# Preparation of a latent-attention layer: six small loads asked behind the compressing weights, and result remainders computed ahead of the splitting of values

## Chip, cores and metric

The kernel runs on 1 core of one Trainium2 chip. The metric is the device time of one execution in microseconds; a kernel's time is the median of its runs.

## What is computed

One layer on 2048 tokens of 512 features in fp32: latent attention with 16 heads, then a linear layer, each followed by a sum with its input and a layer normalisation. Cut to what matters:

```python
cq = rms_norm(x @ w_qa.T, q_a_ln_w)                 # 384 compressed query features
q  = (cq @ w_qb.T), 16 heads of 128 + 64; the 64 are rotated by cos, sin
ckv = x @ w_kva.T                                   # 128 + 64 features
k_pe = rotate(ckv[..., 128:])                       # one rotated key of 64 for all heads
ckv_l = rms_norm(ckv[..., :128], kv_a_ln_w)
kv = ckv_l @ w_kvb.T                                # per head 128 of key, 128 of value
attn = softmax(mask(q @ k.T * scale)); y = (attn @ v) @ w_o.T
x = layernorm(x + y)
x = layernorm(x + (x @ (weight * scale_weight[:, None]).T + bias))
```

The kernel never forms `kv`: it folds `w_kvb` into the query weights and into the output weights, so keys are `ckv_l` (`key_c`) with the rotated `key_pe`, and values are `ckv_l` without its weight (`val`). Each fp32 operand is kept as two parts, the rounded value (hi) and its remainder (lo), and products are made of the parts.

## The kernel before

`build` runs `prepare_phase`, then `attention_phase`. The preparation walks over four chunks `c` of 512 tokens; a chunk has four tiles `t` of 128 tokens, and the folding of one of four groups of heads goes on beside the tiles. On every engine the order is written out by hand; engines meet through counting semaphores.

**Before the chunks.** SyncE (SP) asks for the identity, the compressing weights `wa_rows` (`w_qa`, then 128 rows of `w_kva`, lines 260 and 261, semaphore `wa_loaded`), the tail of `w_kva` (262), chunk 0's angles `cos` and `sin` (`load_angles`, 255), the two norm weights `q_w` and `kv_w` (264, 266), the mask (268) and the FFN's scale (269). GpSimd (POOL) asks for the first tile of tokens, waits for `wa_loaded`, then asks for the second tile, `w_kvb`, `w_qb` (285, 287), two tiles and the output weights. TensorE (PE) waits for `ident` and `wa_loaded` and turns the compressing weights (354, 358); ScalarE (ACT) and VectorE (DVE) copy them out. DVE then casts the mask (584), scales the norm weights (588, 590) and waits for the angles (592); ACT waits for four such steps, `consts_made`, before its first squares (535).

**A tile on each engine.** PE: `project` (392), `turn_x` of the next tile (370), then a few `fill`s of the weight folding (436, 442, 447, 452, 459), between them `project_key` (402), and `turn_results` of the tile before (410, 412, 417); three more fills (`at_end`, 459) and `turn_results(3)` end a chunk. ACT: squares (535, 537), copy of the tokens, `split` hi parts (506, 517, 519), `cq_n` (544), then `hi(t-1)`, the rounding of the turned results into `cq`, `key_c` and `key_pe` (528, 530, 528), and its stores to DRAM (550, 553, 561, 565). DVE: `safe` (621), rotation of the key (631 to 637), remainders of the folded weights (`split`, 601, 603), `c_n` (644), the splitting of the values (`v_hi` 650, `v_lo` 652), and for `t > 0` `lo(t-1)`, the three remainders of the results (611, 613, 611). POOL: the powers (309), the FFN scaling (321) and the loads of the next chunk.

**What waits for `lo`.** The three operations of `lo` count `tok_lo`. PE's `project_key(t)` waits for `3 * (t - 1)` of the chunk, since it overwrites the bank from which `lo` reads; so `project_key(2)` waits for `lo(0)`, which DVE computes in tile 1. `turn_results(3)` waits for `lo(2)`, computed in DVE's tile 3. The store of `cq` (565) waits for `lo(3)`; ACT's `hi(0)` of the next chunk waits for that store's landing (`cq_free`), since it writes into the same `cq`. Nobody in the preparation reads `val`; the attention does.

```python
for t in range(4):
    ...                                   # rotation, split(n) for the tile's fills
    dve.wait_ge(cqn_done, c * 4 + t + 1)
    ...                                   # c_n, then v_hi and v_lo
    if t:
        lo(t - 1)
for n in at_end:
    split(n)
lo(3)
```

Of the kernel before, what the change touches and what calls it, by code (L numbers as in the profile page):

```python
# [39 lines left out]
def chunk(c):  # L40

    return c


def stored(view):

    return view.bitcast(F32)
# [67 lines left out]
def prepare_phase(nc, m, block, x, w_qa, w_kva, w_qb, w_kvb, w_o, q_ln, kv_ln, w_ffn, scale_w, ident_in, mask_in, cos_in, sin_in):  # L115
# [6 lines left out]
    with ExitStack() as ctx:  # L122
        def sem(name):
            return ctx.enter_context(nc.semaphore(name))
# [45 lines left out]
        wa_loaded = sem("wa_loaded")  # L170
# [80 lines left out]
        @block.sync  # L251
        def _(sp):
            def load_angles(c):
                for table, source in ((cos, cos_in), (sin, sin_in)):
                    sp.dma_start(table[:, 4 * chunk(c):4 * chunk(c) + 4, :],
                                 source.rearrange("(t p) d -> p t d", p=P)[:, 4 * chunk(c):4 * chunk(c) + 4, :]
                                 ).then_inc(angles_loaded[c > 0], 16)

            sp.dma_start(m.ident[:, :], ident_in).then_inc(ident_loaded, 16)
            sp.dma_start(wa_rows[:, 0:3, :], w_qa.rearrange("(o p) i -> p o i", p=P)).then_inc(wa_loaded, 16)  # L260
            sp.dma_start(wa_rows[:, 3, :], w_kva[0:C]).then_inc(wa_loaded, 16)
            sp.dma_start(wa_tail[0:DR], w_kva[C:C + DR]).then_inc(tail_loaded, 16)
            load_angles(0)
            sp.dma_start(q_w, q_ln.rearrange("(k p) -> p k", p=P),
                         allow_slow_non_contiguous=True).then_inc(wo_free, 16)
            sp.dma_start(kv_w, kv_ln.rearrange("(k p) -> p k", p=P),
                         allow_slow_non_contiguous=True).then_inc(cq_free, 16)
            sp.dma_start(mask, mask_in).then_inc(wq_free, 16)
            sp.dma_start(ffn_scale, scale_w.rearrange("(o p) -> p o", p=P), allow_slow_non_contiguous=True
                         ).then_inc(m.ffn_free, 16)  # L270
            sp.wait_ge(x_loaded[3], 16)
            for c in range(1, NCH):
                load_angles(c)


            sp.wait_ge(cq_free, 16 * 2)
            load_tokens(sp, m, 1)
# [294 lines left out]
        @block.vector  # L572
        def _(dve):
            nc.vector.memset(minus_half, -0.5).then_inc(consts_made, 1)
            for k in range(1, KH, 2):
                dve.wait_ge(wa_turned, k + 1)
                nc.vector.tensor_copy(wa_t[:, k, 0:QLR + C], m.bank[4 + k]).then_inc(wa_copied, 1)
            dve.wait_ge(wa_turned, KH + 1)
            nc.vector.tensor_copy(wa_t[:, :, QLR + C:WA], TR[:, 0:KH * DR].rearrange("p (k n) -> p k n", k=KH)
                                  ).then_inc(wa_copied, 1)  # L580
            dve.wait_ge(ident_loaded, 16)
            nc.vector.tensor_copy(m.ident16[:, :], m.ident[:, :]).then_inc(consts_made, 1)
            dve.wait_ge(wq_free, 16)
            nc.vector.tensor_copy(m.mask16[:, :], mask).then_inc(consts_made, 1)

            dve.wait_ge(wo_free, 16)
            dve.wait_ge(cq_free, 16)
            nc.vector.tensor_scalar(q_w, q_w, SCALE, None, ALU.mult).then_inc(consts_made, 1)
            dve.wait_ge(m.ffn_free, 16)
            nc.vector.tensor_scalar(ffn_scale, ffn_scale, -1.0, None, ALU.mult).then_inc(ffn_negated, 1)  # L590
            dve.wait_ge(consts_made, 4)
            dve.wait_ge(angles_loaded[0], 32)
            nc.vector.memset(m.small[:, 60:61], 0.0).then_inc(tok_lo, TOK)
            nc.vector.memset(m.small[:, 61:62], 0.0).then_inc(split_lo, SPLITS)
            with dve.Fori(0, NCH) as c:
                def split(n):
                    if fills[n][0] != "turn":
                        src, dst, scale = split_places(n)
                        dve.wait_ge(split_hi, c * SPLITS + split_of[n] + 1)
                        if scale is None:  # L600
                            nc.vector.tensor_tensor(dst(1), src, stored(dst(0)), ALU.subtract).then_inc(split_lo, 1)
                            return
                        nc.vector.scalar_tensor_tensor(out=dst(1), in0=src, scalar=scale, in1=stored(dst(0)),
                                                       op0=ALU.mult, op1=ALU.subtract).then_inc(split_lo, 1)

                def lo(t):

                    for n, (src, dst, scale) in enumerate(token_places(c, t)):
                        dve.wait_ge(tok_hi, c * 12 + 3 * t + max(n, 1) + 1)
                        if scale is None:  # L610
                            nc.vector.tensor_tensor(dst(1), src, stored(dst(0)), ALU.subtract).then_inc(tok_lo, 1)  # L611
                        else:
                            nc.vector.scalar_tensor_tensor(out=dst(1), in0=src, scalar=scale, in1=stored(dst(0)),
                                                           op0=ALU.mult, op1=ALU.subtract).then_inc(tok_lo, 1)

                for t in range(4):
                    b = t % 2
                    tile = chunk(c) * 4 + t

                    dve.wait_ge(squared, c * 8 + 2 * t + 2)  # L620
                    nc.vector.tensor_scalar(safe[:, 2 * b:2 * b + 2], means[:, 2 * b:2 * b + 2], RMS_EPS, None,
                                            ALU.add).then_inc(eps_added, 1)
                    dve.wait_ge(key_ready, c * 4 + t + 1)
                    if t == 3:
                        dve.wait_ge(angles_loaded[1], 32 * (NCH - 1))
                    kp = KP.rearrange("p (a d) -> p a d", a=2)
                    cos_t = cos[:, bass.ds(tile, 1), :].broadcast_to([P, 2, HALF])
                    sin_t = sin[:, bass.ds(tile, 1), :]
                    tc = t_cos.rearrange("p (a d) -> p a d", a=2)
                    ts = t_sin.rearrange("p (a d) -> p a d", a=2)  # L630
                    nc.vector.tensor_tensor(tc, kp, cos_t, ALU.mult).then_inc(rope_parts, 1)
                    nc.vector.tensor_tensor(ts[:, 0:1], kp[:, 1:2], sin_t, ALU.mult).then_inc(rope_parts, 1)
                    nc.vector.tensor_tensor(ts[:, 1:2], kp[:, 0:1], sin_t, ALU.mult).then_inc(rope_parts, 1)
                    dve.wait_ge(rope_parts, c * 12 + 3 * t + 3)
                    kr = k_rot[b].rearrange("p (r a d) -> p r a d", r=2, a=2)
                    for a, op in ((0, ALU.subtract), (1, ALU.add)):
                        nc.vector.tensor_tensor(
                            kr[:, :, a, :], tc[:, a:a + 1, :].broadcast_to([P, 2, HALF]),
                            ts[:, a:a + 1, :].broadcast_to([P, 2, HALF]), op).then_inc(krot_done, 1)
                    for n in beside[t]:  # L640
                        split(n)

                    dve.wait_ge(cqn_done, c * 4 + t + 1)
                    nc.vector.tensor_scalar(c_n[b], PROJ[b][:, QLR:QLR + C], rstd[:, 2 * b + 1:2 * b + 2],
                                            None, ALU.mult).then_inc(cn_done, 1)
                    dve.wait_ge(cn_done, c * 4 + t + 1)
                    v_hi = m.val[:, 0, bass.ds(tile, 1), :]
                    v_lo = m.val[:, 1, bass.ds(tile, 1), :]
                    cn3 = c_n[b].rearrange("p (a d) -> p a d", a=1)
                    nc.vector.tensor_copy(v_hi, cn3).then_inc(val_hi, 1)  # L650
                    dve.wait_ge(val_hi, c * 4 + t + 1)
                    nc.vector.tensor_tensor(v_lo, cn3, stored(v_hi), ALU.subtract)
                    if t:
                        lo(t - 1)
                for n in at_end:
                    split(n)
                lo(3)
# [1374 lines left out]
```

## Time and profile before

| | |
|---|---|
| median of 3 runs | 1716.27 us (1714.79 to 1720.11) |
| the profiled execution's own time | 1716.44 us |
| its span | 1714.7 us |
| TensorE matmul busy in the span | 1679.9 us, 98% |
| DVE, ACT, POOL busy | 1380.5, 1120.8, 979.7 us |
| mean granted TensorE clock | 0.999 |

The profile is of one execution on the one core. The span runs from its first to its last instruction; the execution's own time has 1.74 us more around it. Busy time of PE includes the overlap of pipelined matmuls, so whether PE waits is read from the starts of its groups. The preparation reaches to about 143 us of the span, the attention takes the rest.

### The profile page before, as it was taken

How to read it: one execution, taken by the hardware profiler on the slowest of the kernel's cores; microseconds unless marked ns; L12 is line 12 of the kernel's file. 1: busy time of each engine (PE TensorE's matmuls, PEld its weight loads, DVE VectorE, ACT ScalarE, POOL GpSimd, SP SyncE). 2: the span in 40 equal slices, each digit the busy share in tenths (PEclk: the TensorE clock that was granted, in tenths of full speed). 3: DMA queues.
4: the chain of work that ended last, by engine and by line, in shares of the span. 5: the costliest groups of instructions: out<-in, count | busy, mean ns of one | idle time of the engine just before them, and what ended most of it. 6: DMA issues, size and time to landing. Idle time of an engine off the chain costs nothing.

```text
span 1714.7 us, 28541 instructions
## 1 busy us (share of the span) xinstructions
PE 1679.9 (98%) x8789; PEld 1395.8 (81%) x8789; DVE 1380.5 (81%) x2493; ACT 1120.8 (65%) x2128; POOL 979.7 (57%) x937
## 2 busy tenths in 40 slices
PE   7999999999999999999999999999999999999997
PEld 5567888888888888888888888888888888888775
DVE  3665788888888887878788888888888888888984
ACT  3564676666666676666677666766667777676774
POOL 4333465565555555655566555555556665556785
PEclk9999999999999999999999999999999999999999
DMA  7984322212321412223211413123123111111422
GB/s 204 367 330 136 105 68 62 87 56 88 110 80 37 144 36 81 69 80 117 81 62 44 142 50 92 51 80 114 62 66 105 56 57 62 50 44 44 136 92 80
DMA packets 112175, 164.03 MB, mean 96 GB/s; under 512 B 13600, under 2 KB 83488, under 8 KB 109984
## 3 DMA queue, kind: packets, MB, share of 16 engines
q1 hardware_dynamic: 105296, 125.86, 22.9%
q0 software_dynamic: 4864, 16.26, 3.0%
q10 hardware_dynamic: 1872, 20.19, 2.9%
q8 instruction: 68, 1.11, 0.3%
q14 instruction: 75, 0.61, 0.1%
HBM read 101.19 MB, written 61.08 MB: 95 GB/s over the span
## 4 chain that ended last, share of the span: by engine, by line
PE 89%; POOL 3%; DVE 3%; issue 2%; DMA 1%; ACT 1%; DVEq 0%; SPq 0%; ACTq 0%; POOLq 0%
PE rows L1464 35%; PE bank L1494 7%; PE bank L1497 7%; PE bank L1495 7%; PE rows L1527 7%; PE rows L1427 5%; PE bank L1527 3%; PE rows L392 2%; PE rows L1440 2%; PE bank L1427 2%; PE bank L1484 2%; PE bank L1440 1%; POOL split_p L1730 1%; PE rows L1473 1%; PE rows L1505 1%
## 5 line engine op out<-in xcount | busy, mean ns | idle before, releaser
L1730 POOL TENSOR_TENSOR split_p<-pool,split_p 128x512 fp32r<-128x512 f32 x544 | 703.3, 1294 | 503.2 <-ACT split_p L1618 503.1
L1464 PE MATMUL rows<-q_c,key_c 128*128 128x512 f32 x1632 | 477.0, 400 | 1.4 <-DVE top L1858 1.4
L1606 ACT COPY pool<-rows 128x512 f32<-128x512 f32 x480 | 281.8, 587 | 227.3 <-PE rows L1464 226.6
L1858 DVE TENSOR_TENSOR top<-rows,top 128x512 f32<-128x512 f32 x420 | 288.6, 687 | 124.5 <-ACT pool L1606 121.0
L1873 DVE TENSOR_TENSOR pool<-bank,pool 128x512 f32<-128x512 f32 x544 | 369.7, 680 | 19.8 <-PE bank L1484 19.8
L1611 ACT ACTIVATE pool<-pool 128x512 f32<-128x512 f32 x544 | 345.9, 636 | 18.1 <-DVE pool L1873 17.1
L1618 ACT CAST split_p<-pool 128x512 fp32r<-128x512 f32 x544 | 333.2, 612 | 16.7 <-PE bank L1497 16.7
L1464 PE MATMUL rows<-q_pe,key_pe 128*128 128x512 f32 x1088 | 337.1, 391 | 0.4 <-DMA q_pe<-pe_dram 0.4
L1885 DVE TENSOR_TENSOR bank<-bank,pool 128x512 f32<-128x512 f32 x480 | 330.9, 689 | 0.0
L1464 PEld LDWEIGHTS rows<-q_c,key_c 128*128 128x128 f32 x1632 | 288.0, 189 | 50.0 <-DVE top L1858 5.0
L1464 PEld LDWEIGHTS rows<-q_pe,key_pe 128*128 128x128 f32 x1088 | 204.2, 188 | 46.2 <-DMA q_pe<-pe_dram 0.9
L1497 PE MATMUL bank<-split_p,val 128*128 128x512 f32 x544 | 213.7, 393 | 2.9 <-POOL split_p L1730 2.7
L1494 PE MATMUL bank<-split_p,val 128*128 128x512 f32 x544 | 214.0, 393 | 1.5 <-ACT o_sum L1624 1.0
L1495 PE MATMUL bank<-split_p,val 128*128 128x512 f32 x544 | 212.3, 390 | 0.0
L1527 PE MATMUL rows<-wo,o_t 128*128 128x512 f32 x528 | 127.3, 390 | 0.4 <-ACT o_t L1636 0.4
L1497 PEld LDWEIGHTS bank<-split_p,val 128*128 128x128 f32 x544 | 102.1, 188 | 29.0 <-POOL split_p L1730 7.4
L1494 PEld LDWEIGHTS bank<-split_p,val 128*128 128x128 f32 x544 | 102.1, 188 | 25.9 <-ACT o_sum L1624 3.4
L1735 POOL TENSOR_TENSOR o_t<-o_sum,o_t 128x512 fp32r<-128x512 f32 x64 | 83.0, 1296 | 69.8 <-ACT o_t L1636 69.8
L1495 PEld LDWEIGHTS bank<-split_p,val 128*128 128x128 f32 x544 | 102.2, 188 | 21.2
L1527 PEld LDWEIGHTS rows<-wo,o_t 128*128 128x128 f32 x528 | 98.9, 188 | 21.7 <-issue 1.2
L1636 ACT CAST o_t<-o_sum 128x512 fp32r<-128x512 f32 x64 | 39.7, 621 | 111.4 <-DVE o_sum L1897 97.2
L1427 PE MATMUL rows<-cq,wq 128*128 128x256 f32 x612 | 80.1, 285 | 0.3 <-DVE key_pe L611 0.3
(193 smaller groups left out, 2101.9 us busy)
## 6 DMA issues: line engine op xcount, KB each, us to landing
q_pe<-pe_dram SPq DMA_DIRECT2D x128, 128.0 KB, 2.6
y_dram<-y SPq DMA_DIRECT2D x62, 256.0 KB, 2.1
cq<-cq_dram SPq DMA_DIRECT2D x19, 768.0 KB, 4.9
y<-y_dram SPq DMA_DIRECT2D x48, 256.0 KB, 3.0
pe_dram<-by_sin SPq DMA_DIRECT2D x32, 256.0 KB, 2.1
pe_dram<-by_cos SPq DMA_DIRECT2D x32, 256.0 KB, 2.2
cq_more<-cq_dram SPq DMA_DIRECT2D x10, 768.0 KB, 4.9
table<-table_dram SPq DMA_DIRECT2D x56, 128.0 KB, 2.7
```

The lines of the kernel that those rows point to most:

```text
L1464: mm = pe.matmul(by_head(out), k, q, start=(z == 0), stop=(z == 4))
L1494: pe.matmul(OUT, m.val[:, 0, j, :], split_p[:, n % 2, 0, :], start=(t == 0), stop=False)
L1495: pe.matmul(OUT, m.val[:, 1, j, :], split_p[:, n % 2, 0, :], start=False, stop=False)
L1497: pe.matmul(OUT, m.val[:, 0, j, :], split_p[:, n % 2, 1, :], start=False, stop=(t == keys(it) - 1)).then_inc(values_done, 1)
L1527: mm = pe.matmul(aux(u), o_t[:, a, h * P:h * P + P], m.wo[:, b, h, :], start=(n == 0), stop=(n == 3 * HG - 1))
L1606: nc.scalar.copy(slot(n), SCORES[n % N_SCORES]).then_inc(scores_copied, 1)
L1611: nc.scalar.activation(slot(n), slot(n), ACT.Exp).then_inc(exp_done, 1)
L1618: nc.scalar.copy(split_p[:, n % 2, 0, :], slot(n)).then_inc(p_hi, 1)
L1730: nc.gpsimd.tensor_tensor(split_p[:, n % 2, 1, :], slot(n), stored(split_p[:, n % 2, 0, :]), ALU.subtract).then_inc(p_lo, 1)
L1858: nc.vector.tensor_tensor(out, SCORES[n % N_SCORES], slot(number(it, 0)) if t == 1 else out, ALU.max).then_inc(scores_maxed, 1)
L1873: nc.vector.tensor_tensor(slot(n), MAXES, slot(n), ALU.add).then_inc(shifted, 1)
L1885: nc.vector.tensor_tensor(TOTAL, TOTAL, slot(n), ALU.add).then_inc(summed, 1)
```

## The change

Two edits, both inside `prepare_phase`. SP gets one wait, for both transfers of `wa_loaded`, ahead of `load_angles(0)`; the loads behind it on SP, `q_w`, `kv_w`, mask and FFN scale, stand behind the wait too. On DVE, `lo(t - 1)` moves from behind `v_lo` to between the wait for `cn_done` and `v_hi`. No operation is added or left out.

```diff
--- before.py
+++ after.py
@@ -260,6 +260,7 @@
             sp.dma_start(wa_rows[:, 0:3, :], w_qa.rearrange("(o p) i -> p o i", p=P)).then_inc(wa_loaded, 16)
             sp.dma_start(wa_rows[:, 3, :], w_kva[0:C]).then_inc(wa_loaded, 16)
             sp.dma_start(wa_tail[0:DR], w_kva[C:C + DR]).then_inc(tail_loaded, 16)
+            sp.wait_ge(wa_loaded, 32)
             load_angles(0)
             sp.dma_start(q_w, q_ln.rearrange("(k p) -> p k", p=P),
                          allow_slow_non_contiguous=True).then_inc(wo_free, 16)
@@ -644,14 +645,14 @@
                     nc.vector.tensor_scalar(c_n[b], PROJ[b][:, QLR:QLR + C], rstd[:, 2 * b + 1:2 * b + 2],
                                             None, ALU.mult).then_inc(cn_done, 1)
                     dve.wait_ge(cn_done, c * 4 + t + 1)
+                    if t:
+                        lo(t - 1)
                     v_hi = m.val[:, 0, bass.ds(tile, 1), :]
                     v_lo = m.val[:, 1, bass.ds(tile, 1), :]
                     cn3 = c_n[b].rearrange("p (a d) -> p a d", a=1)
                     nc.vector.tensor_copy(v_hi, cn3).then_inc(val_hi, 1)
                     dve.wait_ge(val_hi, c * 4 + t + 1)
                     nc.vector.tensor_tensor(v_lo, cn3, stored(v_hi), ALU.subtract)
-                    if t:
-                        lo(t - 1)
                 for n in at_end:
                     split(n)
                 lo(3)
```

SP at its start, before and then with the change (lines move by one; `small` holds `q_w`, `kv_w` and the FFN scale, `pool` the mask):

```order
L261 DMA wa_rows<-in_L_attn_w_kva 128x512
L262 DMA wa_tail<-in_L_attn_w_kva 64x512
L255 DMA cos<-const_cos 128x4x32
L255 DMA sin<-const_sin 128x4x32
L264 DMA small<-in_L_attn_q_a_ln_w 128x3x1
L266 DMA small<-in_L_attn_kv_a_ln_w 128x1
L268 DMA pool<-const_mask 128x128
```

```order
L261 DMA wa_rows<-in_L_attn_w_kva 128x512
L262 DMA wa_tail<-in_L_attn_w_kva 64x512
L255 DMA cos<-const_cos 128x4x32 [waits wa_loaded]
L255 DMA sin<-const_sin 128x4x32
L265 DMA small<-in_L_attn_q_a_ln_w 128x3x1
L267 DMA small<-in_L_attn_kv_a_ln_w 128x1
L269 DMA pool<-const_mask 128x128
```

The first load of angles now carries the wait, and the five behind it follow it in the old order.

DVE in a chunk's tile 1, from `c_n` on, before and then with the change:

```order
L644 TENSOR_SCALAR c_n<-rows,small 128x128 [waits cqn_done]
L650 ISA [waits cn_done]
L650 COPY val<-c_n 128x128
L652 ISA [waits val_hi]
L652 TENSOR_TENSOR val<-c_n,val 128x128
L609 REGISTER_ALU
L611 TENSOR_TENSOR cq<-rows,cq 128x3x128 [waits tok_hi]
L613 ISA [waits tok_hi]
L613 SCALAR_TENSOR_TENSOR key_c<-rows,small,key_c 128x128
L611 ISA [waits tok_hi]
L611 TENSOR_TENSOR key_pe<-bank,key_pe 128x128
```

```order
L645 TENSOR_SCALAR c_n<-rows,small 128x128 [waits cqn_done]
L610 REGISTER_ALU [waits cn_done]
L612 TENSOR_TENSOR cq<-rows,cq 128x3x128 [waits tok_hi]
L614 ISA [waits tok_hi]
L614 SCALAR_TENSOR_TENSOR key_c<-rows,small,key_c 128x128
L612 ISA [waits tok_hi]
L612 TENSOR_TENSOR key_pe<-bank,key_pe 128x128
L653 ISA
L653 COPY val<-c_n 128x128
L655 ISA [waits val_hi]
L655 TENSOR_TENSOR val<-c_n,val 128x128
```

The three operations of `lo` now stand in front of both operations on `val`; the two waits of `val` stay, that for `cn_done` now ahead of `lo`. Tiles 2 and 3 read the same, tile 0 has no `lo` and is as it was.

## Rows read from the trace of the kernel before

**Rows 1.** A stretch: us, busy PE, PEld, DVE, ACT, POOL, clock, DMA share, GB/s.
```profile
150.00:1600.00 1450.00, 1447.20 (x7612) 1227.76 (x7611) 1215.62 (x2049) 970.35 (x1799) 841.89 (x697) 1.00 0.25 80
```

**Rows 2.** Waits of PE from 20 to 146 us: us in total, times, longest.
```profile
PE bank L402 <- DVE key_pe L611: 2.0, 3, 1.4
...
PE rows L410 <- DVE key_pe L611: 1.5, 3, 0.6
```

**Rows 3.** DMA from 0 to 6.7 us: packets; an issue, KB, us to landing.
```profile
DMA packets 759, 1.38 MB, mean 206 GB/s; under 512 B 52, under 2 KB 180, under 8 KB 759
...
wa_rows<-in_L_attn_w_kva SPq DMA_DIRECT2D x1, 256.0 KB, 6.1
```

**Rows 4.** DMA from 6.7 to 9 us: packets.
```profile
DMA packets 2361, 0.33 MB, mean 142 GB/s; under 512 B 2172, under 2 KB 2300, under 8 KB 2361
```

**Rows 5.** DMA issue at 9.51 us: KB, us to landing.
```profile
pool<-in_L_attn_w_qb POOLq DMA_DIRECT2D x1, 768.0 KB, 7.9
```

**Rows 6.** Timeline to 20 us: start, us, engine, line, operation, idle before and releaser.
```profile
1.79 0.48 SPq L261 DMA_DIRECT2D wa_rows<-in_L_attn_w_kva  x1
...
5.67 0.49 SPq L269 DMA_DIRECT2D small<-in_L_ffn_scale_weight  x1
...
8.04 3.65 PE L354 MATMUL bank<-ident,wa_rows 128*128 128x128 f32 x16 [8.04 <-DMA wa_rows<-in_L_attn_w_kva]
...
19.26 0.49 ACT L535 ACTIVATE squares<-rows 128x384 f32<-128x384 f32 x1 [5.29 <-PE rows L392]
...
19.50 1.06 PE L436 MATMUL bank<-pool 128*128 128x128 f32 x8
```

**Rows 7.** Timeline, chunk 0, tiles 1 to 3.
```profile
28.77 1.85 DVE L637 TENSOR_TENSOR k_rot<-t_cos,t_sin 128x64 f32<-128x64 f32 x2
...
29.34 1.05 POOL L321 TENSOR_TENSOR ffn_rows<-ffn_rows,small 128x512 f32<-128x512 f32 x1
...
32.19 0.23 DVE L650 CAST val<-c_n 128x128 f32 x1
...
32.77 0.55 DVE L611 TENSOR_TENSOR cq<-rows,cq 128x384 fp32r<-128x384 f32 x1
...
32.93 0.60 PE L452 MATMUL bank<-ident,pool 128*128 128x128 f32 x4
...
33.83 1.10 PE L402 MATMUL bank<-pool,x_t 128*128 128x64 f32 x8 [0.31 <-DVE key_pe L611]
...
43.96 2.80 PE L459 MATMUL bank<-pool 128*128 128x512 f32 x6
...
47.24 2.06 DVE L603 SCALAR_TENSOR_TENSOR wo<-bank,small,wo 128x512 fp32r<-128x512 f32 x3
...
47.38 0.55 PE L410 MATMUL rows<-ident,cq_n 128*128 128x128 f32 x3 [0.61 <-DVE key_pe L611]
...
47.41 0.75 POOL L291 DMA_DIRECT2D pool<-in_L_attn_w_kvb  x1 [1.94 <-PE bank L459]
```

**Rows 8.** The chain that ended last: the store of chunk 0's `cq`.
```profile
51.78 13.73 DMA cq_dram<-cq
```

**Rows 9.** Timeline, chunk 2, then chunk 3.
```profile
96.94 0.37 ACT L530 ACTIVATE key_c<-rows,small 128x128 f32 x1
...
97.80 0.55 DVE L611 TENSOR_TENSOR cq<-rows,cq 128x384 fp32r<-128x384 f32 x1
...
129.07 0.28 DVE L611 TENSOR_TENSOR key_pe<-bank,key_pe 128x128 f32 x1
...
129.37 0.60 PE L452 MATMUL bank<-ident,pool 128*128 128x128 f32 x4
...
129.80 1.00 PE L402 MATMUL bank<-pool,x_t 128*128 128x64 f32 x8
...
139.55 2.74 PE L459 MATMUL bank<-pool 128*128 128x512 f32 x6
...
142.13 0.49 PE L410 MATMUL rows<-ident,cq_n 128*128 128x128 f32 x3
```

## The prediction

> **What bounds the kernel now.** I read, in this order, the stretches, PE's waits in the preparation, the timeline there, and the DMA traffic of the first microseconds. From 150 to 1600 us PE is busy for 1447.2 of 1450 us [rows 1]: that part keeps its length, and what the preparation gains or loses is handed to the end whole. In the preparation PE stands still at its start, until the compressing weights are in [rows 6], and then almost only at two waits, three times each, always for the last operation of `lo` (611) [rows 2]. The edits aim at just these two.
>
> **Part 1, the wait on SP.** `w_kva` is asked at 1.79 us and lands 6.1 us later, at 7.9; PE starts at 8.04, and POOL's next loads hang on the same landing [rows 3, 6]. Up to 6.7 us the DMA engines moved 1.38 MB [rows 3], which is the sum of identity, `w_qa`, 128 rows of `w_kva` and the first tile of tokens (64 + 768 + 256 + 256 KB). So going by bytes the weights could be in at 6.7; they land 1.2 us later. In between lie the six small loads: of 2361 packets from 6.7 to 9 us, 2172 are under 512 B [rows 4]. With the change these packets come after the landing. Bounds: 0 if the last engine's share of `w_kva` simply ended late, 1.2 if the small packets alone hold it back. The few packets of under 512 B before 6.7 (52 of 759 [rows 3]) say that some engines ran ahead and others were still at the large rows, so part of the 1.2 is unevenness that stays. I take **0.5**, a little under the middle. A shift of PE's start moves everything behind it, as POOL's loads start with it.
>
> That nothing of the 1.2 us is due to the small loads is the first rival; no row separates the two. The Trainium skill (DMA: Bandwidth & Descriptors, "Queues, rings and completion order") has a rule that speaks for that rival and against my term: on each DMA engine the descriptors of one issuer are consumed in ring order, so that small loads asked later on the same queue cannot stand in front of `w_kva`, and the sum below would be 1715.1.
>
> What the wait costs: six requests that ended at 6.16 us [rows 6] now start at about 7.9 - 0.5 = 7.4 and, at their old pace of 0.56 us each (seven from 2.27 to 6.16), end at about 10.7. Behind them on SP stand only angles of the later chunks, which wait for a token tile anyway. ACT needs `q_w` and mask before its squares at 19.26 [rows 6]. With a landing of up to 6.1 us [rows 3] after the request the constants are there by about 17, over 1.5 us early after the 0.5 shift: cost 0. The small packets now share the engines with POOL's loads. The one needed first is `w_qb`, asked at 9.51 and landed 7.9 us later, at 17.4 [rows 5]; PE wants it at 19.50 [rows 6]: cover of 2.1 us. Nearly all of the small packets moved within 2.3 us [rows 4], when little else was left, so the delay is at most about that, less what falls in gaps of the POOL loads: cost 0, with its excess in rival 4.
>
> **Part 2, `lo` ahead of `val`.** `v_hi` starts at 32.19 and `lo` at 32.77 [rows 7]: `lo` can start 0.58 us earlier if ACT's hi parts are there. The moved pair ends as late as `lo` ended before, so DVE's next work keeps its start. What each wait costs I take from starts. `project_key(2)` comes 0.90 us behind the four transposes in front of it (32.93 to 33.83 [rows 7]), and 0.43 where nothing is missing (129.37 to 129.80 [rows 9]): 0.47 lost. `turn_results(3)` comes 3.42 us behind three fills (43.96 to 47.38 [rows 7]), 2.58 in chunk 3 (139.55 to 142.13 [rows 9]): 0.84 lost, of which the trace counts 0.61 as idle. Rows 2 leave some 0.9 idle for chunks 1 and 2 together, 0.45 each, by starts about 0.6. Now along the chunks:
> - Chunk 0, key: all of **0.47** goes; 0.58 covers it, and PE itself is late next.
> - Chunk 0, results: 0.58 of the 0.84 goes. But this is given back. The store of `cq` is released by `lo(3)`, behind DVE's three splits from 47.24 [rows 7], which the swap doesn't move. It takes 13.73 us [rows 8], and ACT's `hi(0)` of chunk 1 waits for it, then `lo(0)`, then PE: that key wait is the longest of rows 2 (1.4) and has 0.58 more to wait. Net 0.
> - Chunk 1, key: bound by that store, no gain. DVE now computes `val` behind `lo`, which makes `safe` and POOL's power some 0.7 us late; ACT has three copies to make first, so this is hidden; without that cover it would cost the 0.7.
> - Chunk 1, results: 0.58 gained. Chunk 2, key: the next store lets ACT end `key_c` at 97.31 (96.94 + 0.37), and `lo` began at 97.80 [rows 9]. So `lo` gains only 0.49, some 0.44 with the semaphore's delay. Chunk 1's 0.58 and this wait's 0.47 together yield **0.44**.
> - Chunk 2, results: **0.58** more. Chunk 3, key: PE was not held before (`lo` ended at 129.35, PE came at 129.80 [rows 9]). PE now comes 1.02 earlier against its store, `lo` only 0.44: 129.35 - 0.44 + 0.06 = 128.97 against 128.78, a new wait of **0.19** behind that store.
> - Chunk 3, results and the first attention product: no wait for a moved operation; nothing.
>
> Part 2 gives 0.47 + 0.44 + 0.58 - 0.19 = 1.30; with part 1 1.80. The profiled execution took 1716.44, so 1716.44 - 1.80 = 1714.64, rounded to **1714.6**. The median of the runs, 1716.27, lies 0.17 below the profiled one; I don't correct for that, since the runs spread over 5 us.
>
> **Rivals.**
> 1. *The small loads never held the weights back.* For it, both were asked on SP, the large rows first; against it, the 1.2 us between bytes and landing. 1716.44 - 1.30 = 1715.1. Chance 0.24.
> 2. *The stores don't bind.* If the DMA has room and `cq`'s store moves along with PE, nothing is given back: 0.47 + 0.58 + 0.58 + 0.47 + 0.58, and 0.5: 3.18, so 1713.3. With a part 1 at its upper bound 1712.6. Against it, the 13.73 us of the store. Chance 0.12.
> 3. *DVE and POOL meet at the new place.* In tile 1 the two operations on `k_rot` take 1.85 us for 64 columns each, where one of 128 columns takes 0.23, and end at 30.6, just after POOL's multiply from 29.34 to 30.39 [rows 7]: DVE stood still for POOL. At the chunk's end POOL asks for `w_kvb` at 47.41, for 0.75 us; the pair on `val`, which was long done, will run until about 47.3. If it slips by a few tenths behind POOL, DVE's splits, `lo(3)` and the store come 0.75 later, in three chunks: 2.25 given back of 1.80, 1716.9. Against it, it just ends in time, and POOL is released by the last fill, which moves no earlier than DVE. Chance 0.07. The Trainium skill (SBUF — State Buffer, "Who interferes with whom") says that a DVE copy in a two-port mode and a GpSimd operation block each other for their whole length, and that a DVE operation with two SBUF inputs blocks only against GpSimd's reads; the `k_rot` row agrees with the latter, and by the rule only `v_hi` can be held here, which narrows this rival.
> 4. *Slower: `w_qb` lands late.* Place: PE's first fill at 19.50. It decides once the small packets delay the 17.4 us landing by more than 2.1 us. The longest that a small load can push is taken as the longest landing of rows 3, 6.1 us, beyond which nothing of it is left in the queue: 6.1 - 2.1 = 4.0 us lost, less 1.80: 1718.6. For it, these packets took the 2.3 us of rows 4 with little beside them; against it, that is still only about the cover. Chance 0.05.
> 5. *Nothing arrives at the end*, for one because ACT's first store request ends at its own time and not with PE: 1716.4. Chance 0.07.
>
> **Numbers.** Forecast 0.45, rivals 0.24, 0.12, 0.07, 0.05, 0.07. The range takes in rivals 1, 3 and 5 and most of 2, with the runs' own scatter: 1712.2 to 1717.6. About 0.3%, 5 us, is what a measurement of this kernel can tell from no change. No case reaches it by itself; only scatter or an effect that I don't see does: faster 0.04, same 0.93, slower 0.03.
>
> **What would show it.** Right: PE's first transpose near 7.5 us; the key wait of chunks 0 and 2 at line 403 gone or short, the results wait cut to some 0.3 in chunk 0 and none in 1 and 2; the key wait of chunk 1 longer than 1.4, ended by the store; a short new one in chunk 3; the attention's first product about 1.8 us earlier. Part 1 is wrong if `w_kva` still lands at 7.9; part 2 if `lo` starts within 0.3 us of its old distance from `c_n`, or if the store of `cq` lands earlier against the chunk's start than 13.7 us behind an unmoved `lo(3)`. The forecast as a whole is wrong if the first attention product moves by less than 0.5 or more than 3.

## The result, and the profile after

The changed kernel takes **1721.34 us** (median of 15 runs, 1719.09 to 1724.77), the kernel before on the same chip 1714.84 (15 runs, 1713.90 to 1720.11). The ratio is 1.0035, with a 95% interval of 1.0027 to 1.0043: slower by 6 us, outside the predicted range (1712.2 to 1717.6) and on the side that had 3 chances in 100.

| | before | after |
|---|---|---|
| profiled execution's own time | 1716.44 us | 1719.09 us |
| span | 1714.7 us | 1717.3 us |
| PE busy | 1679.9 us | 1679.6 us |
| DVE, ACT, POOL busy | 1380.5, 1120.8, 979.7 us | 1380.9, 1120.5, 979.6 us |
| mean granted clock | 0.999 | 0.997 |

The work is the same; something waits. PE's waits from 20 to 146 us in the profile of after (what waited, for what, us in total, times, longest):

```profile
PE bank L437 <- DVE small L595: 3.9, 1, 3.9
PE bank L403 <- DVE key_pe L612: 3.0, 3, 1.9
PE bank L418 <- DVE t_sin L634: 0.9, 1, 0.9
```

Against [rows 2], the results wait (1.5, now at line 411) is gone, the key wait has grown from 2.0 to 3.0, and a wait of 3.9 is new: PE's first fill waits for line 595, the preset of `split_lo` on DVE. The timelines of the same profile show what DVE and PE did (start, us, engine, line, operation, idle before and its releaser), SP's requests first:

```profile
7.70 0.39 SPq L255 DMA_DIRECT2D cos<-const_cos  x1
...
9.75 0.43 SPq L269 DMA_DIRECT2D pool<-const_mask  x1
10.23 0.43 SPq L270 DMA_DIRECT2D small<-in_L_ffn_scale_weight  x1
```

```profile
17.44 0.23 DVE L585 CAST mask<-pool 128x128 bf16<-128x128 f32 x1 [4.79 <-DMA pool<-const_mask]
...
21.02 0.17 DVE L591 TENSOR_SCALAR small<-small 128x4 f32<-128x4 f32 x1 [3.27 <-DMA small<-in_L_ffn_scale_weight]
...
21.19 0.06 DVE L595 MEMSET small<- 128x1 f32 x1
```

```profile
16.85 0.60 PE L371 MATMUL rows<-ident,pool 128*128 128x128 f32 x4
21.30 1.35 PE L437 MATMUL bank<-pool 128*128 128x128 f32 x8 [3.85 <-DVE small L595]
22.45 1.81 PE L403 MATMUL bank<-pool,x_t 128*128 128x64 f32 x8
24.05 2.72 PE L437 MATMUL bank<-pool 128*128 128x128 f32 x16
```

The FFN's scale, 2 KB that only POOL needs, and only in tile 1, is asked at 10.23 and used at 21.02. Everything behind it on DVE stands, the two presets with it. How long each request took is in the DMA issues from 6 to 12 us (KB, us from issue to landing):

```profile
pool<-in_L_attn_w_qb POOLq DMA_DIRECT2D x1, 768.0 KB, 8.4
...
pool<-const_mask SPq DMA_DIRECT2D x1, 64.0 KB, 7.7
...
small<-in_L_attn_kv_a_ln_w SPq DMA_DIRECT2D x1, 0.5 KB, 4.6
small<-in_L_ffn_scale_weight SPq DMA_DIRECT2D x1, 2.0 KB, 10.8
```

Before, the scale landed 4.3 us after its request, which stood at 5.67 [rows 6]. By single microseconds (packets, MB, share of the 16 engines), SP's queue (q1) goes from hundreds of packets to a trickle beside POOL's large loads (q0). From 10 to 11 us it still has 648, from 20 to 21 only the scale's last 3:

```profile
q1 hardware_dynamic: 648, 0.06, 48.2%
...
q0 software_dynamic: 93, 0.38, 100.0%
q1 hardware_dynamic: 3, 0.00, 0.2%
```

The wait of 3.85 is not its whole price. PE's first fill starts 1.80 us later than before (21.30 against 19.50 [rows 6]), but tile 1's `project` 3.53 later (26.60 against 23.07). In between the granted clock fell (columns: stretch, busy PE, PEld, DVE, ACT, POOL, clock, DMA share, GB/s):

```profile
20.00:22.00 2.00, 0.70 (x6) 0.70 (x7) 0.40 (x4) 0.00 (x0) 0.38 (x1) 1.00 1.03 381
22.00:23.00 1.00, 1.00 (x9) 1.00 (x7) 0.00 (x0) 0.23 (x1) 0.91 (x2) 0.57 1.04 311
23.00:25.00 2.00, 2.00 (x10) 2.00 (x10) 0.55 (x4) 0.46 (x1) 0.00 (x0) 0.50 1.14 279
```

0.50 is the lower of the two levels, 1.2 GHz; the 16 products at 24.05 took 2.72 us, where 2.00 is usual (21.23 us in before).

For the rest one table of starts serves, from the profiled execution of each kernel (us): PE's first transpose, the first fill, `project` of chunk 0's tiles 1 and 3 (behind the key wait), of chunk 1's tiles 0 (behind `turn_results(3)`) and 3 (behind its key wait), of chunk 3's tile 3, and the span. "Before, again" is the unchanged kernel in a later run; it shows by how much two executions of one kernel differ.

| kernel | PE start | fill | c0 t1 | c0 t3 | c1 t0 | c1 t3 | c3 t3 | span |
|---|---|---|---|---|---|---|---|---|
| before | 8.04 | 19.50 | 23.07 | 36.64 | 48.02 | 70.19 | 132.50 | 1714.7 |
| before, again | 7.84 | 17.31 | 20.92 | 34.49 | 45.80 | 67.97 | 130.29 | 1712.1 |
| after | 7.81 | 21.30 | 26.60 | 39.60 | 50.77 | 73.50 | 135.60 | 1717.3 |
| after, again | 7.92 | 23.80 | 29.76 | 42.75 | 53.69 | 76.48 | 138.79 | 1720.6 |
| wait only | 8.00 | 19.67 | 24.98 | 38.54 | 50.21 | 72.39 | 134.70 | 1716.8 |
| order only | 8.12 | 17.14 | 20.75 | 33.74 | 44.22 | 68.13 | 131.55 | 1713.2 |
| presets first | 8.26 | 18.40 | 22.04 | 35.03 | 45.74 | 69.64 | 131.71 | 1713.5 |
| scale first | 8.19 | 17.82 | 21.50 | 34.49 | 45.68 | 69.60 | 131.11 | 1714.3 |
| POOL after scale | 7.85 | 19.26 | 22.90 | 35.89 | 46.93 | 71.35 | 132.87 | 1714.6 |
| busy wait, 9 | 7.67 | 24.38 | 27.95 | 40.99 | 51.88 | 78.00 | 139.02 | 1721.6 |
| busy wait, 4 | 8.43 | 23.43 | 27.00 | 40.19 | 50.99 | 77.73 | 139.63 | 1721.4 |
| cq store first | 8.30 | 17.57 | 21.21 | 34.78 | 45.72 | 66.82 | 129.12 | 1710.8 |
| change, cq store first | 8.37 | 20.31 | 25.62 | 38.61 | 49.73 | 70.26 | 130.83 | 1713.8 |
| order, cq store first | 8.00 | 17.28 | 20.92 | 33.91 | 44.51 | 65.04 | 125.61 | 1708.6 |

From chunk 3's tile 3 to the end of the span the kernels differ by under 2 us (1581.7 to 1583.2), so what the preparation loses arrives, as [rows 1] said. The first row is itself a late execution: its first `project` took 5.20 us, that of "before, again" 3.70 at the same granted clock of 1.00, and its first fill came 2.2 later. Measured from the second row, after is late by 4.0 at the first fill, 5.7 at tile 1 and 5.2 in the span, near the 6 us of the medians.

### The profile page after: what moved, and what is told of

The parts are those of the page before. It is cut to its first block, busy times and chain, and to the rows that moved or that the text cites. A ratio compares the mean times of both kernels' runs of the same rounds, so it can differ in the third digit from the quotient of the medians.

```text
span 1717.3 us, 28541 instructions
## 1 busy us (share of the span) xinstructions
PE 1679.6 (98%) x8789; PEld 1397.0 (81%) x8789; DVE 1380.9 (80%) x2493; ACT 1120.5 (65%) x2128; POOL 979.6 (57%) x937
## 4 chain that ended last, share of the span: by engine, by line
PE 88%; POOL 3%; DMA 3%; DVE 2%; issue 2%; ACT 1%; SPq 0%; ACTq 0%; DVEq 0%; POOLq 0%
PE rows L1465 35%; PE bank L1495 7%; PE bank L1498 7%; PE bank L1496 7%; PE rows L1528 7%; PE rows L1428 6%; PE bank L1528 3%; PE bank L1428 2%; PE rows L1441 2%; DMA cq_dram<-cq 2%; PE bank L1485 2%; PE bank L1441 1%; POOL split_p L1731 1%; PE rows L393 1%; PE rows L1474 1%
## 5 line engine op out<-in xcount | busy, mean ns | idle before, releaser
L1612 ACT ACTIVATE pool<-pool 128x512 f32<-128x512 f32 x544 | 346.1, 636 | 18.1 <-DVE pool L1874 17.2
```

Of the source, the lines that this page charges most:

```text
L1612: nc.scalar.activation(slot(n), slot(n), ACT.Exp).then_inc(exp_done, 1)
```

## Experiments

The theory after the result: the scale lands late behind SP's wait, holds DVE's presets and so PE's first fill, and the fallen clock adds to it. Its rivals: the order on DVE costs something; `w_qb` is late; the profile shows an odd execution.

**The change again, and each part alone.** The two parts are the two hunks of the diff above, one in each kernel.

> The changed kernel once more, for a second profile. My theory: the six small loads, asked next to the large loads of POOL, land late; the last, the FFN scale (10.8 us to landing in the first profile), holds DVE at line 591, DVE's presets of tok_lo and split_lo stand behind it, and PE's first fill (437) waits for them, 3.9 us, after which its granted clock is 0.50 for some 3 us. The first profile was of 1719.1 us, the median is 1721.3: by this theory the landing differs from run to run, so a profile of 1721 us or more shows the scale landing at 22 us or later and the first fill 2 us or so later than 21.30. Rival: the first part costs a fixed 3.5 us and the rest of the 6.5 us is lost in the attention; then the first fill stands near 21.3 in this profile too, and the loss grows behind 160 us. Time 1721.3, 1720.3 to 1722.5.

> The wait on SP alone, DVE in its old order. My theory: the whole loss and 1.0 us more, since the reordering gave back 1.0 in the first profile (PE's lag fell from 3.53 at tile 1 of chunk 0 to 2.5 in the attention): 1722.3, with PE's first fill held by DVE at 595 as before. Rival (the reordering is what costs): about 1714.8 or less.

> lo ahead of val alone, without the wait on SP. My theory: 1.0 us less than before, 1713.8; key wait of chunk 0 gone, results waits of chunks 0 to 2 0.6 shorter, key waits of chunks 1 and 2 longer by what was gained, as the stores of cq bind. Rival (the stores don't bind here): 2.7 us less, 1712.1. Rival (the reordering costs): over 1716.

| kernel | median us (runs) | before beside it | ratio, 95% |
|---|---|---|---|
| after, again | 1720.96 (6) | 1715.41 (22) | 1.0030 (1.0018 to 1.0042) |
| wait only | 1721.90 (5) | 1715.41 | 1.0038 (1.0024 to 1.0051) |
| order only | 1715.85 (11) | 1715.41 | 1.0000 (0.9991 to 1.0009) |

The whole loss is the wait on SP; the new order, from which I had expected 1713.8 alone, is worth nothing that can be measured. In the second profile of after the scale landed even later, as the chain that ended last shows (start, us, what):

```profile
10.33 13.15 DMA small<-in_L_ffn_scale_weight
```

PE had been ready since about 17.4 and the first fill came at 23.80; `w_qb` had landed 7.9 us after its request, as in [rows 5]. With the wait alone the scale took 8.9, and the fill waited 2.45:

```profile
19.67 1.16 PE L437 MATMUL bank<-pool 128*128 128x128 f32 x8 [2.45 <-DVE small L595]
```

**The presets ahead of the waits.** The constants come no earlier; DVE only sets the two counters before it waits for them.

```diff
+            nc.vector.memset(m.small[:, 60:61], 0.0).then_inc(tok_lo, TOK)
+            nc.vector.memset(m.small[:, 61:62], 0.0).then_inc(split_lo, SPLITS)
             dve.wait_ge(ident_loaded, 16)
...
             dve.wait_ge(consts_made, 4)
             dve.wait_ge(angles_loaded[0], 32)
-            nc.vector.memset(m.small[:, 60:61], 0.0).then_inc(tok_lo, TOK)
-            nc.vector.memset(m.small[:, 61:62], 0.0).then_inc(split_lo, SPLITS)
```

> The changed kernel with DVE's presets of tok_lo and split_lo moved ahead of its waits for identity, mask, norm weights, scale and angles. My theory: PE's first fill waits only for w_qb (landed at 17.7 in the first profile) and starts near 17.7 instead of 21.3, no fall of the clock; DVE is still held by the scale until about 21, but its work of tile 0 is not needed on PE before 24. 1712 (before less 1.8 and less 1.0). Rival (the scale's late landing delays something that counts anyway, safe or the first remainders): the first fill moves but PE waits at tile 1; 1716 to 1721.

1714.54 (11 runs), ratio 0.9996 (0.9987 to 1.0005): the whole 6 us are back (I had expected 1712), though the scale still takes 9.0 us. DVE, then PE:

```profile
18.05 0.23 DVE L587 CAST mask<-pool 128x128 bf16<-128x128 f32 x1 [4.79 <-DMA pool<-const_mask]
...
19.74 0.17 DVE L593 TENSOR_SCALAR small<-small 128x4 f32<-128x4 f32 x1 [1.39 <-DMA small<-in_L_ffn_scale_weight]
```

```profile
18.40 1.13 PE L437 MATMUL bank<-pool 128*128 128x128 f32 x8 [0.44 <-issue]
```

The fill starts 1.3 us before the scale is there, as `w_qb` lands (8.6 us after its request at 9.72), and the clock stays up: tile 1 comes 3.64 behind it (before: 3.57). So the preset is what carried the late scale to PE.

**The scale asked ahead of the wait.** Its request moves in front of `sp.wait_ge(wa_loaded, 32)`; the other five stay behind it.

```diff
+            sp.dma_start(ffn_scale, scale_w.rearrange("(o p) -> p o", p=P), allow_slow_non_contiguous=True
+                         ).then_inc(m.ffn_free, 16)
             sp.wait_ge(wa_loaded, 32)
```

> The changed kernel with the FFN scale asked ahead of the wait, behind the tail of w_kva; angles, norm weights and mask stay behind the wait. My theory: the loss is the scale's landing at the end of the six; it now lands by 10 us, and the last of the other five, the mask (7.7 us to landing in the changed kernel), holds DVE until 16.7 to 18.3, so the first fill waits 0 to 1 us: 1715, with PE's start unmoved near 8.0. Rival (any small load behind the wait lands late, whichever is last): the mask or the angles take the scale's place at 20 us and more, 1720.

1716.99 (11 runs), ratio 1.0008 (0.9999 to 1.0017): most comes back, perhaps not all. The mask, now the last request behind the wait, was cast at 17.25, 0.6 ahead of the fill at 17.82; its cover is thin, and other executions (1714.71 to 1719.94) may have lacked it. That last is an inference from one profile and the spread.

**POOL's weights behind the scale.** This tries the cause of the lateness itself: POOL asks for `w_qb` only once the scale is in.

```diff
             load_kv(0, 0)
+            pool.wait_ge(m.ffn_free, 16)
             load_wq_rows(0)
```

> The changed kernel with POOL waiting for the FFN scale's landing before it asks for the rows of w_qb and all behind. My theory: the small loads are late because each small packet takes its turn with the large ones of POOL's loads; with only 512 KB of these beside them the scale lands within 6 us of its request, by 16.5 us, not after 9 to 13; w_qb then lands at 23 to 25 and holds the first fill instead: 1721 to 1725. Rival (a small load of 512 packets behind a wait is slow by itself): the scale lands at 19 us or later all the same.

A single run: 1716.92. With `w_qb` and the loads behind it held back, the same 2 KB, asked at 10.26, landed after 3.1 us, and `w_qb`, asked at 13.65, after 5.5, where the other profiles with the wait have 7.7 to 9.2:

```profile
small<-in_L_ffn_scale_weight SPq DMA_DIRECT2D x1, 2.0 KB, 3.1
```

```profile
pool<-in_L_attn_w_qb POOLq DMA_DIRECT2D x1, 768.0 KB, 5.5
```

`w_qb` was there at 19.2, not at 23 to 25 as I had expected, and so was the first fill (19.26); the time came out 4 us under my forecast. The scale's lateness is thus the company of POOL's loads; that rests on one profile, with a landing far outside the others. Beside them the scale took 8.7 to 13.2 us in the seven profiles that asked for it there last, without them 3.1. The Trainium skill (DMA: Bandwidth & Descriptors, "Queues, rings and completion order") says that each DMA engine takes turns between the queues that have work for it, a packet of descriptors at a time; the trickle of q1 beside a full q0 agrees with that, but no run shows the turns themselves.

**The wait filled with work.** To price the clock alone, dummy products stand in chunk 0's tile 0 behind `turn_x`; they write a bank that is not in use, and chunk 0 is written out of the loop. The short version has `range(4)`.

```diff
                         turn_x(c, t + 1)
+                    if first and t == 0:
+                        for _ in range(9):
+                            pe.matmul(m.bank[5], x_t[0][:, 0:P], wa_t[:, 0, 0:QLR + C], start=True, stop=True)
```

> The changed kernel, with nine further products of 128x512 on PE in chunk 0 alone, between the turning of tile 1's tokens and the first fill (3.9 us at 0.43 each; they read the first tile's tokens and write a bank that the first fill overwrites; chunk 0 is written out ahead of the loop for it). My theory: PE's wait for DVE's presets costs twice, once the wait itself and once the granted clock of 0.50 behind it (some 1.7 to 2.4 us over the next 25 products). The nine products lie inside the wait, so the first fill starts no later than before, and the clock stays at 1.00: 1719.3, 2 us under the changed kernel. Rival (the half clock is no cost of its own, PE would be held by ACT and DVE there anyway): 1721.3.

> The changed kernel with four further products on PE in the wait instead of nine. The nine took 7.89 us and not 3.9, since each product of 128x512 passes twice at 0.43: they outlasted the wait, though the granted clock stayed at 1.00. Four take 3.5 us and end at about 20.5. My theory: where the scale lands at 20 to 21 us, PE's first fill starts as in the changed kernel and the 25 products behind it run at full clock, 1.7 to 2.4 us gained: 1719.3. Rival: no gain, 1721.

Nine took 1724.68 (5 runs), ratio 1.0053 (1.0040 to 1.0067); four took 1722.53 (5 runs), 1.0036 (1.0022 to 1.0050). As a gain both missed. Each product passed twice, so the nine took 7.89 us, twice what I had reckoned, and the four began only at 19.99, behind a first `project` of 5.21; the scale was in at 19.7 and 19.6, and in both the fill came over 3 us after it. But that is not where these two kernels fall behind the changed one. At chunk 1's tile 0 they are only 0.2 (four) and 1.1 us (nine) later than in the first profile of after, at its tile 3 already 4.2 and 4.5, about the 4.1 and 4.3 of the spans. Chunk 0's store of `cq` took 15.1 and 14.5 us there, not 13.7, PE's key wait grew to 3.44 and 2.83 us, and the clock behind it was at 0.50. Why the store took longer no run shows. With four dummies:

```profile
72.33 1.97 PE L403 MATMUL bank<-pool,x_t 128*128 128x64 f32 x8 [3.44 <-DVE key_pe L616]
```

As a price the two kernels answer, since the stretch behind the first fill stands apart from that. PE and the clock there with four dummies:

```profile
19.99 3.60 PE L469 MATMUL bank<-pool,x_t 128*128 128x512 f32 x8
23.43 1.05 PE L437 MATMUL bank<-pool 128*128 128x128 f32 x8
```

```profile
24.00:26.00 2.00, 2.00 (x21) 2.00 (x20) 0.48 (x4) 0.69 (x1) 0.00 (x0) 1.00 1.12 304
```

From the first fill to tile 1 both took 3.57 us, as before, though the fill was as late as in after's profiles. Where PE had stood still it took 5.30 (after, 3.85 idle), 5.31 (wait only, 2.45 idle), 5.31 (change with the store first, 2.83 idle) and 5.96 (after again, 6.43 idle). So the idle wait costs **1.7 to 2.4 us** more than its length, and it costs that at 2.45 idle as at 3.85.

**The unchanged kernel again.**

> The kernel before once more, for a second profile. My theory: in its first profile the first eight products of line 392 took 5.20 us, in all runs since 3.70, with PE's start unmoved; that is a difference between executions and not of the change, so here the products may take 3.70, with PE ahead by 1.5 to 2.3 at 20 us and by 1 or less in the attention. 1715.3. Rival (the slow first products belong to this kernel alone): 5.20 us again.

1714.95 (11 runs), ratio 0.9999 (0.9990 to 1.0008). PE's waits are those of [rows 2] (key 2.0, longest 1.4; results 1.5, longest 0.6). The first `project` took 3.70 us, and PE started at 7.84.

**The store of `cq` ahead of that of `wo`.** Order only gained 0.58 by chunk 0's tile 3 and another 0.83 by chunk 1's tile 0, measured from "before, again" and the fills (34.49 - 33.74 - 0.17; then 45.80 - 44.22 less those). Behind the next key wait it was 0.16 late. PE, then the clock there:

```profile
64.16 1.10 PE L402 MATMUL bank<-pool,x_t 128*128 128x64 f32 x8 [1.95 <-DVE key_pe L611]
65.11 2.17 PE L452 MATMUL bank<-ident,pool 128*128 128x128 f32 x12
```

```profile
62.00:64.00 2.00, 0.22 (x2) 0.00 (x0) 0.90 (x3) 1.68 (x8) 0.00 (x0) 1.00 0.45 140
64.00:66.00 2.00, 1.84 (x15) 1.84 (x16) 1.16 (x8) 1.17 (x3) 1.15 (x2) 0.93 0.98 328
66.00:68.00 2.00, 2.00 (x11) 2.00 (x11) 0.23 (x2) 1.61 (x4) 1.93 (x4) 0.50 0.49 101
```

The store went out 1.02 earlier than in "before, again" (48.55 against 49.57), took as long (13.75 against 13.73), and the key came 1.01 earlier (64.16 against 65.17). But PE, ready earlier still, idled 1.95 instead of 1.37, and behind that the clock was at 0.50, which cost 1.2 by tile 3 (3.97 from the key's start against 2.80). The next experiment takes that wait away: ACT stores `wo`, 2 MB, just ahead of `cq`, and nobody waits for `wo` so early.

```diff
-                if not last:
-                    act.wait_ge(split_lo, SPLITS + c * SPLITS + SPLITS)
-                    act.dma_start(m.wo_dram[c], words(m.wo)).then_inc(wo_free, 16)
                 hi(3)
                 if not last:
                     act.wait_ge(tok_lo, TOK + c * TOK + TOK)
                     act.dma_start(m.cq_dram[chunk(c)], words(m.cq)).then_inc(cq_free, 16)
+                    act.wait_ge(split_lo, SPLITS + c * SPLITS + SPLITS)
+                    act.dma_start(m.wo_dram[c], words(m.wo)).then_inc(wo_free, 16)
```

> lo ahead of val alone (no wait on SP), and on ACT the store of cq asked ahead of the store of wo at a chunk's end. My theory: the reordering's gain is given back at the key waits of chunks 1 to 3, where ACT waits for the store of cq (9.6 us in three waits in the order-only run), and the long wait in chunk 1 also halves the granted clock. With cq's 1.5 MB ahead of wo's 2 MB the store lands some 5 us earlier, no ACT wait for it, no long key wait: 4 us less than order alone, 1711.5. Rival (the store's landing isn't what holds, or wo's later store holds something else): no gain, 1715.5 or more.

> The kernel before with only the store of cq asked ahead of the store of wo. My theory: the longest key wait (1.4 us idle, chunk 1) shrinks to the 0.3 to 0.5 that DVE's order causes, chunks 0 and 2 keep theirs, results waits keep theirs: 1.1 us less than before, 1714; so the two edits together (1710.1) gain more than the sum of each alone, since the store gives back what the order gains. Rival (all 5.7 us of the two edits are the store's): 1710.5.

> The whole change with the store of cq asked ahead of the store of wo. My theory: nothing but the wait on SP separates it from the 1710.1 us of order and store without that wait, and with the stores out of the way the start's lag reaches the end whole: 5 to 7 us more, 1716. Rival (the lag at the start is partly absorbed later): 1713 or less.

| kernel | median us (runs) | before beside it | ratio, 95% |
|---|---|---|---|
| new order on DVE, `cq` store first | 1710.09 (7) | 1715.78 (23) | 0.9968 (0.9957 to 0.9980) |
| `cq` store first | 1713.82 (11) | 1714.94 (21) | 0.9991 (0.9982 to 1.0001) |
| the change, `cq` store first | 1716.09 (11) | 1714.94 | 1.0004 (0.9994 to 1.0013) |

With the new order and without SP's wait this is a version that beats both kernels. DMA issues from 45 to 55 us of it:

```profile
wo_dram<-wo ACTq DMA_DIRECT2D x1, 2048.0 KB, 15.2
cq_dram<-cq ACTq DMA_DIRECT2D x1, 1536.0 KB, 10.3
```

`cq` lands in 10.3 us instead of 13.7 [rows 8] and `wo` in 15.2 instead of 12.0. PE's key and results waits are gone; its longest waits from 20 to 146 us are

```profile
PE bank L417 <- DVE t_sin L632: 0.3, 1, 0.3
PE rows L1426 <- DVE key_pe L610: 0.2, 1, 0.2
```

With the store alone in the old order the key wait is 0.9 and the results wait still 1.5. The parts are worth little each (0.0000 and 0.0009 of the time, both within noise) and 0.0032 together. The waits listed say why: each removes one of two waits that would take the other's place. The last kernel has the change's loss at the first fill (2.83 idle and a fallen clock) and makes most of it good later: against "before, again" it is 4.7 late at tile 1 (25.62 - 20.92) and 1.7 in the span.

## Why the prediction was wrong

- **What bounds the kernel: right.** What the preparation lost (5.3 at chunk 3's tile 3, from "before, again") arrived (5.2 in the span).
- **Part 1, gain of 0.5: wrong, it is 0.** PE started between 7.67 and 8.43 in the nine profiles with the wait, between 7.84 and 8.30 in the five without it. In after `w_kva` landed at 7.68 instead of 7.90, but the landing varies by more than that within either group (7.5 to 8.3 us, and 7.7 to 8.2). Rival 1 was right: the 1.2 us between bytes and landing was not the small packets' doing. The rule of the Trainium skill that spoke for it (DMA: Bandwidth & Descriptors, "Queues, rings and completion order") agrees with these starts.
- **Part 1, cost: the step that failed.** It reads "With a landing of up to 6.1 us [rows 3] after the request the constants are there by about 17, over 1.5 us early after the 0.5 shift: cost 0". The last constant took 10.8 and 13.15 us and was there at 21.0 and 23.5. I had bounded a landing beside POOL's loads by one from before most of those loads began, although [rows 5] showed 7.9 for a load among them; even 7.9 would have been too small. The second half of the miss is that I named ACT's squares as the only reader. `split_lo`'s preset, behind the same waits on DVE, was not in the sum, so a fill that needs no constant waited for the least urgent of them. The squares themselves began at 17.93 in after, behind the landing of the mask, against 17.07 in "before, again".
- **Part 1, the covers: read from a late execution.** The 19.26 and 19.50 against which I set both landings come from the profile with the first `project` of 5.20 us. In "before, again" the squares start at 17.07 and the first fill at 17.31, just behind `w_qb`'s landing at 17.2. So the covers of over 1.5 and of 2.1 us were nearly nothing in such an execution, and 12 of the 14 profiles are of that kind.
- **Part 1, the clock: not in the sum.** Behind the wait it added 1.7 to 2.4 us. Delay and clock together give the 6 us, which "presets first" takes away whole.
- **Rival 4: right in sign, wrong in mechanism.** `w_qb` landed 8.4 us after its request, at 17.7, which would have cost some 0.4 against the first fill of "before, again", not 6; and the rival was put at 1718.6, nearly 3 us short.
- **Part 2, the waits: right in part; net: wrong.** The key wait of chunk 0 went as forecast (0.58 measured by starts, 0.47 forecast). The results wait went whole and brought 0.83; I had 0.58 and then "net 0", because `lo(3)` would stay. It did not stay: the store moved 1.02 along with PE. The longer key wait in chunk 1 came as said (1.4 to 1.9), but what took the gain back there was the clock behind it. Chunk 2's key wait, which was to yield 0.44, grew instead from 0.31 to 0.75. The short new wait of chunk 3, forecast at 0.19, was 1.10 long in order only and 0.16 in after. The measured worth is 0 (0.9991 to 1.0009, or 1.5 us either way, which does not exclude the 1.30 by itself); in the profile the way from the first fill to chunk 3's tile 3 took 114.4 us with the new order and 113.0 without it.
- **Rivals 2, 3 and 5.** Rival 2 was right that the store moves with PE, and wrong that it then doesn't bind; only with the store's own place changed does it stop binding. Of rival 3's stopped DVE no wait in the profiles speaks. Rival 5 is near the truth for part 2 alone, by another mechanism.
- **Open:** whether the last 0.0008 of "scale first" is the mask; why the first `project` takes 5.20 us in two of the 14 executions and 3.7 in the others (in the slow ones its first weight loads take 0.34 us instead of 0.19, as they do elsewhere at a recorded clock of 0.50, but the record here says 1.00); why the store of `cq` took longer in the kernels with dummy products; and why the clock fell behind a key wait of 1.9 in order only and not in after, below.

## What to carry to other kernels

When a small load is moved behind a wait, list every instruction that stands behind its readers on their engine, presets of counters among them, and put what needs no data ahead of the first wait. Take its landing time from a row in which the same large transfers run beside it, not from a quiet stretch, and the reader's time from more than one execution, since a cover of 2 us was 0.1 us in the next. And price a wait of the matmul engine with the clock it may lose, and two waits in a row (here results and store) together: each edit alone showed nothing, both gave 0.3%.

## What the runs showed of the hardware that I had not expected

- A load of 2 KB asked last on a queue landed 8.7 to 13.2 us later beside another queue's large loads (seven profiles), 3.1 us later with `w_qb` and the loads behind it held back (one).
- The granted clock fell to 0.50 (1.2 GHz) at the first fill in all four profiles with an idle wait there of 2.45 us or more. It stayed at 1.00 behind the 1.43 us of "POOL after scale", and where dummy products filled the wait.
- Behind the key wait of chunk 1 the length of the wait alone did not decide. The clock fell in order only (1.95 us, above), presets first (1.91), scale first (2.00) and POOL after scale (1.97), and not in after (1.94) and after again (1.99). After's 12 products take 1.48 us, where order only has 2.17:

```profile
70.70 1.10 PE L403 MATMUL bank<-pool,x_t 128*128 128x64 f32 x8 [1.94 <-DVE key_pe L612]
71.64 1.48 PE L453 MATMUL bank<-ident,pool 128*128 128x128 f32 x12
```

- Chunk 0's store of 1.5 MB took 13.70 to 13.79 us behind that of 2 MB on the same queue in nine profiles, 14.5 and 15.1 in the two with dummy products, and 10.2 to 10.4 in front of it in three.
